# Local attention in array quarters: 128 keys a query, query length inside the exponential, weights divided before they are turned

## The reference

```python
DIM, DEPTH, HEADS, DIM_HEAD, WINDOW = 128, 2, 8, 64, 64      # x: (4, 1024, 128)
h = shift_token(x)                 # features 64..127 are taken from the token before
q, k, v = split(h @ wqkv[l])       # 3 x 512 columns, 8 heads of 64
q = l2norm(q) * q_scale            # unit length over the 64 of a head
k = l2norm(k) * k_scale
q, k = rotary_xpos(q, k)           # q * cos * s + rotate_half(q) * sin * s ; k with 1 / s
# blocks of 64 queries; each sees its own block and the block before it
sim = einsum('bhwid,bhwjd->bhwij', q * 8.0, look_around(k))      # 64 x 128
mask = (i < j) | (i > j + WINDOW) | (j == -1)
attn = softmax(where(mask, -max, sim))
o = einsum('bhwij,bhwjd->bhwid', attn, look_around(v))
x = x + o @ wo[l]                  # then a gated feed-forward, local_ffn
```

## Time and profile before

| | us |
|---|---|
| the three timed runs | 4980.36, 4974.6, 4959.91 |
| their median | 4974.6 |
| the profiled execution's own time | 4973.73 |
| its span in the trace | 4971.9 |

### The profile page before, as it was taken

The page is one execution under the profiler, slowest core; times in us unless marked ns, Lnnn a source line. Parts: engine busy times, 40 slices in busy tenths (PEclk is TensorE's granted clock), DMA queues, the critical chain, the costliest instruction groups (busy, mean ns, idle before and its releaser), DMA issues. The chain is left out here.

```text
span 4971.9 us, 52722 instructions
## 1 busy us (share of the span) xinstructions
PE 3709.0 (75%) x19990; PEld 1790.0 (36%) x19990; DVE 3088.1 (62%) x4888; ACT 2705.7 (54%) x3832; POOL 1087.2 (22%) x1105
## 2 busy tenths in 40 slices
PE   6695777888858989889879997899777696621125
PEld 4372111111112222222227775677643263211114
DVE  4123878888436565655558885788757132368876
ACT  2120566667659989899976763576533222212224
POOL 1302471010021010100003230223110503118770
PEclk9796999999869989999989999999988898865557
DMA  4011131010011000100000000000020011530001
GB/s 127 24 32 40 35 48 27 14 27 14 1 42 26 13 13 13 26 13 13 1 15 1 1 1 6 16 1 1 6 72 0 34 54 33 68 48 0 9 0 31
DMA packets 110183, 117.88 MB, mean 24 GB/s; under 512 B 20476, under 2 KB 81896, under 8 KB 109928
## 3 DMA queue, kind: packets, MB, share of 16 engines
q1 hardware_dynamic: 101736, 97.71, 9.2%
q0 software_dynamic: 8192, 16.79, 1.5%
HBM read 65.62 MB, written 33.82 MB: 20 GB/s over the span
## 5 line engine op out<-in xcount | busy, mean ns | idle before, releaser
L429 PE MATMUL PS<-t 48*128 48x512 bf16 (+1 forms) x3072 | 799.5, 408 | 303.3 <-ACT t L540 126.4
L540 ACT ACTIVATE t<-PS 128x512 f32<-128x512 f32 x1024 | 553.7, 595 | 257.1 <-PE PS L429 253.2
L582 DVE TENSOR_REDUCE t<-PS 128x1 f32<-128x1024 f32 x512 | 621.5, 1221 | 114.6 <-PE PS L421 103.9
L643 DVE TENSOR_TENSOR t<-t 128x1536 f32<-128x1536 f32 (+1 forms) x384 | 586.0, 1588 | 163.9 <-ACT t L558 101.7
L429 PEld LDWEIGHTS PS<-t 48*128 48x128 bf16 (+1 forms) x3072 | 160.8, 95 | 1187.2 <-ACT t L540 459.6
L499 PE MATMUL PS<-t 128*9 128x512 f32 x4096 | 566.2, 627 | 8.0 <-DVE t L643 7.7
L558 ACT ACTIVATE t<-PS,t 128x1536 f32<-128x1536 f32 (+1 forms) x384 | 503.7, 1420 | 30.3 <-PE PS L429 27.5
L560 ACT ACTIVATE t<-PS 128x1536 f32<-128x1536 f32 (+1 forms) x384 | 477.5, 1311 | 58.9 <-PE PS L429 48.2
L1615 POOL TENSOR_TENSOR t<-t 128x512 f32<-128x512 f32 x128 | 225.0, 1777 | 1204.4 <-DVE t L1545 1204.4
L421 PE MATMUL PS<-t 48*128 48x512 bf16 x1024 | 361.5, 406 | 38.2 <-DVE t L582 20.8
L2360 PE MATMUL PS<-t 128*128 128x32 f32 x256 | 61.1, 403 | 392.0 <-ACT t L2395 297.2
(11 more groups left out here) (373 smaller groups left out, 7011.3 us busy)
## 6 DMA issues: line engine op xcount, KB each, us to landing
t<-scr SPq DMA_DIRECT2D x384, 64.0 KB
scr<-t SPq DMA_DIRECT2D x96, 128.0 KB
t<-t SPq DMA_DIRECT2D x16, 512.0 KB, 10.6
scr<-t SPq DMA_DIRECT2D x2, 2560.0 KB
t<-scr SPq DMA_DIRECT2D x16, 320.0 KB, 3.6
scr<-t SPq DMA_DIRECT2D x16, 320.0 KB, 2.7
t<-in_L_ffn_rg_dram SPq DMA_DIRECT2D x8, 256.0 KB, 6.2
t<-in_L_ffn_ru_dram SPq DMA_DIRECT2D x8, 256.0 KB, 6.0
```

The lines of the kernel that those rows point to most:

```text
L429: return e.op.matmul(PS[:, bk, :], Kx[p // 4 % 2][lo:lo + KS, j, kb * 128:kb * 128 + 128], Qx[p // 4 % 2][lo:lo + KS, j, hf * 512:hf * 512 ...
L540: e.op.activation(P[x % 4][:, 2 * hf + side, :], PS[:, 4 + hf, :], ACT.Exp, scale=S8).then_inc(*PW.up((p, k, side, hf)))
L582: e.op.tensor_reduce(MX[p % 2][:, side, qc:qc + 1], PS[:, 2 * side:2 * side + 2, :].rearrange("p a n -> p (a n)"), AX, ALU.max).then_inc(* ...
L643: e.op.tensor_tensor(o, o, SGM[(12 * p + 3 * blk + ti) % 3][:, 0:nu, :], ALU.mult).then_inc(*DG.up((p, blk, ti)))
```

## The change

`local_attention` is written anew; the functions around it are untouched. What it does:

- Keys: a query block of 64 is scored against exactly its own 64 keys and the 64 before. The keys of eight chunks lie in one tile `KT`, chunks in falling order, so that a block's two key blocks are reached by one strided pattern (`keys`). A head's chunk is two products, each on a quarter of the array (64 rows, 64 columns), 128 streamed columns. Scores need banks 3 and 4 instead of 0 to 3; projections keep 0 and 1, values get 2, all else a ring of 5 to 7.
- Lengths: the keys are scaled to unit length after the rotation; the queries are not. The query's length goes into the exponential as its scale, and into the negated maximum. Roots are taken for two chunks at once.
- Weights: the exponential also gives its sum over the keys (`accum_out`). VectorE takes the reciprocal, and GpSimd divides the weights of all heads (128 x 1024) before TensorE turns them: 8 transposes for each chunk.
- Values: they are the loaded operand (64 columns), and the turned weights stream (64 columns), so the product comes out turned; the result's division and transposes are gone. Since a block's first 64 keys must be the block before, SP moves two halves of values by DMA within SBUF into `VA` for each chunk (128 KB each).
- Order: each engine has an order of its own in the rounds, chunks up to six rounds deep (38 rounds). Only the first group of four chunks is turned ahead; the others are turned in the rounds, one group in every fourth. `wqkv` has its own signal, `wo` is loaded last, and the sine table is built before the cosine table.

Of the diff, cut to the core:

```diff
+            QKB, VB, SB = 0, 2, 3
+            W1 = sig("local_w1_in")
+            MOVED = [sig(f"values_moved{i}") for i in range(3)]
...
+                def lengths(n):
+                    return R[n // 2 % 3][:, 16 * (n % 2):16 * (n % 2) + 16]
+                def keys(n, g, k, x):
+                    p = 7 - n % 8
+                    if x:
+                        return KT[g:g + 64, k, p, :, :]
+                    blocks = KT[g:g + 64, k, :, :, :].rearrange("p c w n -> p (c w) n")
+                    return blocks[:, 2 * p:2 * p + 2, :] if n % 8 == 0 else blocks[:, 2 * p:2 * p + 4:3, :]
...
+                    for n in range(NC):
+                        e.wait_ge(AC, ("v", n))
+                        if n > 2:
+                            e.wait_ge(PM, ("pv", n - 3))
+                        e.op.dma_start(VA[n % 3][0:64, :], V[n % NV][0:64, :]).then_inc(*MOVED[n % 3].up(n, 16))
+                        if n % 8:
+                            e.op.dma_start(VA[n % 3][64:128, :], V[(n - 1) % NV][64:128, :]).then_inc(
+                                *MOVED[n % 3].up(n, 16))
...
+                    for what, n in rounds(("scores", 4), ("pT", 5), ("v", 0), ("qkT", 3), ("pv", 5), ("proj", 0),
+                                          ("turn", 0), ("out", 5)):
...
+                                g = 64 * (h % 2)
+                                for x in range(2):
+                                    t = e.op.matmul(
+                                        PS[64 * x:64 * x + 64, SB + h % 2, 128 * (h // 2):128 * (h // 2) + 128],
+                                        QT[i][g:g + 64, h // 2, 64 * x:64 * x + 64], keys(n, g, h // 2, x),
+                                        start=False, stop=h > 5)
...
+                            for u in range(2):
+                                e.wait_ge(AC if u else DV, ("pT", n, u))
+                                for k in range(2 * u, 2 * u + 2):
+                                    for x in range(2):
+                                        for h in (2 * k, 2 * k + 1):
+                                            t = e.op.matmul(
+                                                PS[64 * (h % 2):64 * (h % 2) + 64, b,
+                                                   128 * k + 64 * x:128 * k + 64 * x + 64],
+                                                (V[n % NV] if x else VA[n % 3])[:, 64 * h:64 * h + 64],
+                                                PT[i][:, h, 64 * x:64 * x + 64], start=True, stop=True)
...
+                    for what, n in rounds(("proj", 1), ("pT", 5), ("scores", 4), ("qkT", 3), ("pv", 5), ("v", 0),
+                                          ("turn", 0), ("root", 1)):
...
-                                u, o = 2 * (h % 2) + h // 4, 192 * ((h // 2) % 2)
-                                e.op.activation(PB[i][:, h, 64:256], PS[:, u, o:o + 192], ACT.Exp,
-                                                bias=mx[i][:, h:h + 1]).then_inc(*AC.up(("exp", n, h)))
+                                e.op.activation(PB[i][:, h, :], PS[:, SB + h % 2, 128 * (h // 2):128 * (h // 2) + 128],
+                                                ACT.Exp, bias=mx[i][:, h:h + 1], scale=lengths(n)[:, h:h + 1],
+                                                accum_out=su[i][:, h:h + 1]).then_inc(*AC.up(("exp", n, h)))
...
+                    for what, n in rounds(("unit", 3), ("y", 6), ("sum", 1), ("scores", 4), ("pT", 5), ("cos", 1),
+                                          ("qkT", 3), ("share", 4), ("add", 1), ("turn", 0)):
...
+                        elif what == "add":
+                            e.wait_ge(PO, ("sin", n))
+                            then().tensor_tensor(T1[n % 3][:], T1[n % 3][:], SN[i][:], ALU.add).then_inc(
+                                *DV.up(("rot", n)))
+                        elif what == "unit":
+                            if n % 2 == 0:
+                                r = R[n // 2 % 3]
+                                e.wait_ge(AC, ("root", n // 2))
+                                e.op.tensor_scalar(r[:], r[:], 1e-12, None, ALU.max).then_inc(*DV.up())
+                                then().reciprocal(r[:], r[:]).then_inc(*DV.up(("lengths", n // 2)))
+                            k3 = T1[n % 3][:, 512:1024].rearrange("p (h d) -> p h d", h=8)
+                            then().tensor_tensor(k3, k3, lengths(n)[:, 8:16].unsqueeze(2).broadcast_to([128, 8, 64]),
...
+                            then().scalar_tensor_tensor(out=mx[i][:], in0=mx[i][:], scalar=-1.0, in1=lengths(n)[:, 0:8],
+                                                        op0=ALU.mult, op1=ALU.mult).then_inc(*DV.up(("max", n)))
+                        elif what == "share":
+                            e.wait_ge(AC, ("exp", n, 7))
+                            e.op.reciprocal(su[i][:], su[i][:]).then_inc(*DV.up(("share", n)))
...
+                    for what, n in rounds(("sin", 1), ("share", 4)):
...
+                        else:
+                            e.wait_ge(DV, ("share", n))
+                            e.op.tensor_tensor(PB[i][:], PB[i][:], su[i][:].unsqueeze(2).broadcast_to([128, 8, 128]),
+                                               ALU.mult).then_inc(*PO.up(("p", n)))
```

## The result

| | before | after |
|---|---|---|
| median (lowest to highest), us | 4976.02 (4959.91 to 4980.36) | 4834.68 (4829.5 to 4836.11) |
| the profiled execution / its span, us | 4973.73 / 4971.9 | 4836.11 / 4834.3 |
| ratio of the times | | 0.972, 95% interval 0.9697 to 0.9743 |

I measure a call of the stage as before: from the issue of `wqkv` to the first exponential (head), from there to the first exponential of the last chunk (31 intervals), and from there to the end of the last residual (tail).

What follows compares the result with a forecast made beforehand. TensorE was taken as the bound, busy 12.67 of each 13.35 us round. After: 30 + 28 x 11.5 + 3 x 9.5 + 12.5 = 393 us a call, 56.5 less, twice, giving 4861 us; range 4765 to 4945.

Steps and rivals of the forecast that it cites:

- TensorE's sum of 9.5: TensorE's work per round after the change: 5.9 + 1.8 for scores + 1.8 for values, between 7.7 and 12.9 us.
- The other engines: Work per round after the change: VectorE about 8 us, ScalarE about 9, GpSimd 4.8.
- The exponentials: Eight on ScalarE per round, 0.46 us each, 3.7 in all; bounds 3.1 (2.75 if PSUM reads are cheaper) and 4.9.
- The chain over the port: From last exponential through reciprocal, sum, GpSimd's division, keys, residual, lengths, maximum, negation to the exponentials: 7.7 + 3.7 = 11.4 us a round.
- rival A: VectorE isn't held by the division; TensorE and ScalarE bound at about 10 us a round, 4774 us; chance 0.20.
- The small steps of every second round: Floor and reciprocal of the lengths, raising the round's chain from 11.4 to 11.5 us.
- The last three intervals: The call's last rounds, which lack lengths, sums or keys: 9.5 us each.
- Transfers at nothing: SP's 2 x 128 KB moves within SBUF per round cost nothing; they would have to take over 20 us to show.
- B: Rival: exponentials at their upper end, 4.9 us, in the same chain; 12.6 us a round, 4931 us; chance 0.17.
- C: Rival: array parts don't overlap and narrow loads take a full slot; 14.2 us a round, 5041 us; chance 0.09.
- D: Rival: such losses in part, or a falling granted clock; 13.1 to 13.4 us a round, gain within 25; chance 0.07.

Runs made afterwards that it cites:

- the doubled masks: The kernel before with every mask product made twice in each chunk; ratio 1.0074 to the kernel before.
- the scores by quarter: The changed kernel with its 32 score instructions ordered one quarter of the array after the other; ratio 0.9775 to the kernel before.
- the kernel by logarithm: The combined kernel with the reciprocal root written as exp(-0.5 ln x); ratio 0.9708 to the kernel before.
- the combined kernel: The changed kernel with the sum ahead of the reciprocal, sine behind the negation and `wo` on its own signal; ratio 0.9642 to the kernel before, 0.9658 again.

## Why the prediction was right, and where it was not

**TensorE bounded**: shown by the doubled masks.

**TensorE's sum of 9.5** was too high by 1.5 us, in the two terms that I had called unknown. Scores were put at half of serial, 1.8, and took 1.03; values at a slot of half a load, 1.8, and took 1.09. For the first I had reasoned that the two instructions of an f32 product on one part can't overlap. The starts bear that out, 109 ns apart on one quarter against the 0.107 that I reckoned; what was wrong is the halving that I drew from it. While one quarter works on an instruction, the three others work too, and the time is close to the 0.9 that I had named for four quarters at once. That nothing hangs on it was right: TensorE could lose 1.5 us in three rounds of four. The sign "near 9.5 us busy" came out all the same (8.57 to 9.85), since recorded lengths are longer than the distances that I had added. The values also speak on against the rule that I cited from the Trainium skill (TensorE: Matmul & The Clock Gate, Part 3), by which each would pay load and stream in turn: 0.034 us holds both.

**The other engines.** VectorE was put at about 8, and its 9.47 less the 1.72 that the sum waits for the port are 7.75 (the terms I listed add to 8.5, though, not 8); ScalarE at 9 took 9.05, GpSimd at 4.8 took 4.64.

**The exponentials**, taken at 3.7 us, took 3.50, and 3.66 to the reciprocal. Their spacing of 0.435 instead of 0.46 lies between the bounds, and the cost of the sum was 0.09 each, not a whole smallest instruction.

**The chain over the port** was right in its steps, and 0.9 too long in its sum: against 11.4 a round stood 10.48 in the round shown, of which 0.14 belong to the sine. The division was put at 2.4 and the sum at 1.23 behind it, 3.63 together, and both were done in 2.97; most of this is the division's 1.90 (the row of 128x4096 scaled to 2.3 was too dear), the rest that the sum's own work is 1.07 once it has the port. Residual, lengths and maximum each start 0.1 before the recorded end of what they follow, which makes up the rest. The sign that I named for it was wrong, however: the keys' product "near 2 us" never came, it took 0.69 throughout, which I had named as the sign of rival A. GpSimd won the port before the sum, not after it, and the sum was the victim. The two orders have the same length, so the number held, which is luck and not foresight; a reader who looked at the keys alone would have ruled for A.

**A chain that the forecast didn't have**: copy of queries and keys, sine (2.5 us), negation. In this kernel it costs 0.23 us in every fourth round and 0.05 to 0.16 where the clock falls, 2.3 us in the 31 intervals, and it decides what the next step is worth.

**The small steps of every second round** were sized 0.1 on average and cost 0.7 in each round with a root (floor, reciprocal and their gaps, 2757.69 to 2758.28, and the sine behind them), 0.36 on average. The turned group costs 0.74 in every fourth round, 0.19 on average, where I had 0.2 on VectorE but nothing in the chain.

So the first 28 intervals averaged 10.86 where 11.5 was forecast, 17.8 us less. Three terms went the other way. **The last three intervals**, put at 9.5 each, took 11.79, 11.24 and 10.49, 5.0 more; the granted clock was 0.86, 0.70 and 0.84 in them, and with the scores by quarter, where more of TensorE's work stands there, they took 6.7 more still in the first call. **The head** took 35.1 instead of 30. Its rows:

```profile
2570.97 0.43 DVE L1565 SCALAR_TENSOR_TENSOR t<-t 128x256 f32<-128x256 f32 x1 [5.26 <-DMA t<-in_L_ffn_wo_dram]
...
2579.72 7.75 POOL L1653 TENSOR_TENSOR t<-t 128x512 f32<-128x512 f32 x4 [1.44 <-ACT t L1508]
...
2597.00 1.07 DVE L1626 SCALAR_TENSOR_TENSOR t<-t 128x8 f32<-128x8 f32 x1
```

VectorE's tables wait for the last load of the shared signal, `wo`, which they don't use; then four sines on GpSimd (the second and third chunk's) and VectorE stand in each other's way (7.75 us instead of 5.0, a floor of 32 elements at 1.23), and the negation waits 0.9. I had named the wait for the loads and given it no price. It is the lesser part, 0.65 us: with the sine behind the negation the head is 34.4, and with `wo` on its own signal too it is 34.1. In the kernel by logarithm the third chunk's sines happen to start only behind VectorE's sum and its bound of the lengths (the floor here); these take 1.23 and 0.17 instead of 2.26 and 1.23, its head has no reciprocal, and it lasts 31.6 (32.8 in the second call). So meetings at the port account for some 2 us of the 5; the rest was not tried singly. **The tail** of 12.9 was forecast at 12.5; TensorE runs there at its lower level (0.76 in the last 46 us), so the last transposes and values take 1.97 each instead of 1.1. The terms' errors thus cancel in part: 17.8 too much, 5.0, 5.1 and 0.4 too little, 7.3 us in the first call. Of the 26 us between forecast and median 13 lie in the two calls, and 11.5 in the stages that I had taken as unchanged.

**Transfers at nothing** was right: no engine is recorded as waiting for a moved half, and the transfers land in 2.3 us (KB each, median us from issue to landing):

```profile
t<-t SPq DMA_DIRECT2D x136, 128.0 KB, 2.3
```

**Rivals.** A (no lock) is out by the sum of 2.95 us. Its number fits the combined kernel instead, where neither chain is held up at the port: rounds of 9.1 to 11.2, 10.1 on average (314.4 / 31), where A had 10. B is out at 0.435 us. C and D are out by the slots of 0.032 and 0.034. In D's doubt there was a piece of truth: the granted clock in the stage fell from 0.98 to 0.92, though in the steady rounds of this kernel that cost under 1 us a call; in the kernel with the sum ahead it cost 0.9 in each such round.

## What to carry to other kernels

When the bounding engine is relieved, write down the chain that closes over a round and the time of every step, and look for its twin: two chains here finished within 0.25 us of each other in every steady round, so single edits gave 10 and 2 us a call and both together 23, while lengthening one cost most of what was added. Before a two-input VectorE operation on SBUF is placed beside a GpSimd one, decide which shall go first; moving a 1.23 us sum ahead of the division took 1.7 us off it in every round. Read rounds together with their granted clock, as a fall can look like a round of another kind: once one chain was shortened, 0.6 to 0.9 us in some rounds came from it. And name as evidence the length of the chain, not which of two operations will be the one held up.

## What the runs showed of the hardware

GpSimd and VectorE passed the shared port in turn, whole instruction by whole instruction: with the division twice 1.90 for the first, 1.07 more for the sum recorded with 2.95, 1.76 more for the second division recorded with 2.88, and 0.55 more for the keys recorded with 2.27. Even an operation on 8 elements waited up to 0.9 us. The Trainium skill (SBUF — State Buffer, two separate sides) says that the shared pair of ports is a lock which whoever starts first, GpSimd or a VectorE instruction that needs it, holds for the whole instruction while the other blocks; the trace agrees with these numbers.

Instructions of small f32 products on alternating quarters of the array came 3.3 times as fast as the rate of full products makes them (0.032 against 0.107 us), and 2.4 times as fast as the same ones sorted by quarter. On one quarter they stood 109 ns apart in both orders; with the quarters alternating, four started within 20 ns. Those of 128 x 64 on alternating column halves took 0.034 us each, loads included.

TensorE's granted clock fell to its 1.2 GHz level for parts of an otherwise busy stage. In the round shown the engine had stood idle for 2.02 us, until 2762.52; behind that four products of 512 columns took 3.06 us instead of 1.98. ScalarE waited for them, the sine began later, and the round took 10.48 us instead of 10.34. The same gap of 2.02 us, in the round of 2631.09 for one, was also followed by a clock of 1.00, so the gap alone doesn't tell. What a fall costs depends on whether TensorE's work lies in the longest chain: 0.05 to 0.16 us in the changed kernel, nothing with the sine behind the negation, 0.9 with the sum ahead, 0.6 in the combined kernel. In the kernel with the scores by quarter, where TensorE is busy for 1.5 us more, the clock stayed at its 2.4 GHz level from the third to the 28th round of the first call; that kernel ran on another chip, and the reason was not tested.
